# Left sweeps: GpSimd's residual additions in pieces of 256 columns, one per half step, released by VectorE's remainder

## The reference, cut to what matters

```python
x = x + L0(_gn(x))      # a convolution whose weights are mixed per sample
x = x + L1(_gn(x))      # four sweeps: down, up, right, left
x = x + L2(_gn(x))      # linear attention and a depthwise convolution
x = x + L3(_gn(x))      # four sweeps again
```

```python
def step(prev, row):
    new = row + jax.nn.relu(_conv1d(prev, w, b))   # 64 -> 64 channels, 9 taps
    return (new, new)
```

## Time and profile before

| what | value |
|---|---|
| median of three runs | 3067.09 us |
| the profiled execution: its own time | 3078.55 us |
| its span in the trace | 3076.7 us |
| TensorE busy (matmul) | 2698.7 us, 88% |
| VectorE busy | 2166.5 us, 70% |
| ScalarE busy | 1361.2 us, 44% |
| GpSimd busy | 298.9 us, 10% |
| mean granted TensorE clock | 0.945 of full speed |

### The profile page before, as it was taken

How to read it: one execution, slowest core, us unless ns; L and a number is a source line. 1 busy time by engine, 2 the same in 40 slices (tenths; PEclk the granted TensorE clock), 3 DMA queues, 4 the chain that set the end, 5 groups by cost and what they waited for, 6 DMA issues and landing times. The chain is left out here.

```text
span 3076.7 us, 71764 instructions
## 1 busy us (share of the span) xinstructions
PE 2698.7 (88%) x25712; PEld 2429.3 (79%) x25712; DVE 2166.5 (70%) x5168; ACT 1361.2 (44%) x2113; POOL 298.9 (10%) x816
## 2 busy tenths in 40 slices
PE   5888879999999999928978888886999999999791
PEld 4666669999999999923457676666999999999791
DVE  7888856776667677767028887886766767677865
ACT  2777642246642222236445565652225663222120
POOL 1112110000000011135000100010000000000602
PEclk9998989999999999958989999998999999999695
DMA  4333320000000000079247888777000000000759
GB/s 91 83 83 87 91 113 0 0 0 0 0 0 0 0 0 0 0 222 230 48 42 88 108 101 101 98 91 120 0 0 0 0 0 0 0 0 0 124 94 130
DMA packets 735623, 164.91 MB, mean 54 GB/s; under 512 B 728208, under 2 KB 728848, under 8 KB 730640
## 3 DMA queue, kind: packets, MB, share of 16 engines
q1 hardware_dynamic: 608640, 132.08, 24.8%
q10 hardware_dynamic: 126864, 31.19, 6.2%
HBM read 96.13 MB, written 67.11 MB: 53 GB/s over the span
## 5 line engine op out<-in xcount | busy, mean ns | idle before, releaser
L271 PE MATMUL L_conv<-L_x_hi,L_w_hi 128*128 128x248 f32 (+2 forms) x5040 | 1218.1, 279 | 51.1 <-DVE L_w_lo L234 29.1
L271 PE MATMUL L_conv<-L_x_hi,L_w_lo 128*128 128x248 f32 (+2 forms) x5040 | 1209.7, 279 | 0.0
L158 ACT ACTIVATE L_row_b<-S,L_bias 128x256 f32 (+1 forms) x1008 | 513.4, 510 | 1120.2 <-DVE L_x_hi L212 1109.8
L271 PEld LDWEIGHTS L_conv<-L_x_hi,L_w_hi 128*128 128x128 f32 x5040 | 959.1, 190 | 55.3 <-issue 29.2
L271 PEld LDWEIGHTS L_conv<-L_x_hi,L_w_lo 128*128 128x128 f32 x5040 | 960.6, 191 | 0.0
L222 DVE SCALAR_TENSOR_TENSOR S<-L_conv,L_neg_bias,L_row_b 128x256 f32 x1008 | 487.3, 483 | 446.1 <-PE L_conv L276 445.8
L276 PE MATMUL L_conv<-L_x_lo,L_w_hi 128*128 128x248 f32 (+2 forms) x5040 | 750.8, 279 | 6.6 <-DVE L_x_lo L214 6.6
L276 PEld LDWEIGHTS L_conv<-L_x_lo,L_w_hi 128*128 128x128 f32 x5040 | 659.5, 191 | 10.3 <-DVE L_x_lo L214 9.9
L214 DVE TENSOR_TENSOR L_x_lo<-S,L_x_hi 128x256 fp32r<-128x256 f32 x1016 | 466.5, 459 | 34.7
L212 DVE TENSOR_SCALAR L_x_hi<-S 128x256 fp32r (+1 forms) x1016 | 320.8, 316 | 41.4 <-PEq L47 6.2
L607 PE MATMUL dc_conv<-dc_xz_hi,dc_w_hi 128*128 128x512 f32 x384 | 170.8, 445 | 6.5 <-DVE dc_w_lo L734 6.5
(11 more groups left out here) (202 smaller groups left out, 2829.1 us busy)
## 6 DMA issues: line engine op xcount, KB each, us to landing
dc_raw<-x SPq DMA_DIRECT2D x32, 512.0 KB, 6.6
x_scratch<-dc_raw SPq DMA_DIRECT2D x16, 1024.0 KB, 7.5
at_res<-x_scratch SPq DMA_DIRECT2D x32, 512.0 KB, 11.7
x_scratch<-at_res SPq DMA_DIRECT2D x64, 256.0 KB, 5.8
fs_buf<-x_scratch SPq DMA_DIRECT2D x32, 512.0 KB, 6.7
sh_G<-x_scratch ACTq DMA_DIRECT2D x56, 256.0 KB, 6.0
out<-fs_buf SPq DMA_DIRECT2D x32, 256.0 KB, 4.4
out<-fs_buf ACTq DMA_DIRECT2D x32, 256.0 KB, 4.8
```

The costliest lines, as they stand in the source:

```text
L158: nc.scalar.activation(row_b[p][:, :, :], line(k, at_step(k, i), p), ACT.Identity, bias=bias[:, k:k + 1]).then_inc(row_b_ready[p], 1)
L271: nc.tensor.matmul(out[:, to, :], w[:, k, s * P:(s + 1) * P], x_hi[p][:, at, :], start=(s == PADJ and n == 0), stop=False)
```

## The change

Both classes take a function `split_done(i, p)` instead of the semaphore `new_ready`: it makes GpSimd wait for `lo_ready[p]` of step `i` in the left sweep, that is, until VectorE has written the remainder of that half step. Every addition is cut by rows into pieces of 256 elements per partition, and each piece waits for a half step of its own.

In L1's left sweep a quarter's five additions become ten pieces (16 of the 32 row pairs each). Piece `half` of sample `n` waits for half step (15 + n, half), (31 + n, half) or (47 + n, half). The statistics wait for twice the count. In L3's left sweep an item becomes four pieces (`PIECES`, 8 row pairs each), and the 64 pieces wait for the half steps (31, 0), (31, 1), (32, 0) and so on up to (62, 1), the sweep's last. SP waits for four pieces before it stores an item. Nothing is changed in `final_sum`.

```diff
             if final:
-                final.early_pool(pool, new_ready, done_before)
+                def split_done(i, p):
+
+                    pool.wait_ge(lo_ready[p], turns_before(3, i) + 2)
+
+                final.early_pool(pool, split_done)
...
-    def add_quarter(self, eng, n, g):
+    def add_quarter(self, eng, n, g, rows=slice(0, J)):
         part = slice(g * QUARTER, (g + 1) * QUARTER)
-        cells = self.xr[n][:, :, part]
-        return eng.tensor_tensor(cells, cells, columns_of(self.S, n)[:, :, part], ALU.add)
+        cells = self.xr[n][:, rows, part]
+        return eng.tensor_tensor(cells, cells, columns_of(self.S, n)[:, rows, part], ALU.add)
...
-    def early_pool(self, pool, new_ready, done_before):
+    def early_pool(self, pool, split_done):
         for n in range(RING):
             pool.wait_ge(self.x1_in[n], 16)
         for g in (3, 2, 1):
-            for p in range(2):
-                pool.wait_ge(new_ready[p], done_before(3, STEPS - g * QUARTER))
             for n in range(RING):
-                self.add_quarter(self.nc.gpsimd, n, g).then_inc(self.quarter_summed, 1)
+                for half in range(2):
+                    split_done(STEPS - g * QUARTER + n, half)
+                    self.add_quarter(self.nc.gpsimd, n, g, slice(half * J // 2, (half + 1) * J // 2)).then_inc(self.quarter_summed, 1)
...
-                dve.wait_ge(self.quarter_summed, (3 - g) * RING + n + 1)
+                dve.wait_ge(self.quarter_summed, 2 * ((3 - g) * RING + n + 1))
...
+PIECES = 4
...
-            sp.wait_ge(self.early_summed, item + 1)
+            sp.wait_ge(self.early_summed, PIECES * (item + 1))
...
-    def early_pool(self, pool, new_ready, done_before):
-        for p in range(2):
-            pool.wait_ge(new_ready[p], done_before(3, STEPS - PART))
+    def early_pool(self, pool, split_done):
         for item in range(B):
             pool.wait_ge(self.loaded[item % BUFS], 16 * (item // BUFS + 1))
-            self.add(self.nc.gpsimd, item).then_inc(self.early_summed, 1)
+            for piece in range(PIECES):
+                split_done(STEPS - PART + (item * PIECES + piece) // 2, piece % 2)
+                self.add(self.nc.gpsimd, item, slice(piece * J // PIECES, (piece + 1) * J // PIECES)).then_inc(self.early_summed, 1)
```

More of the change, by code:

```diff
@@ L1769, in store, with add @@
                           self.buf[item % BUFS][q * HALF:(q + 1) * HALF, :, :]).then_inc(self.stored[item % BUFS], 16)
-    def add(self, eng, item):
-        buf = self.buf[item % BUFS]
-        return eng.tensor_tensor(buf[:, :, :], buf[:, :, :], columns_of(self.S, item % B)[:, :, self.columns(item)], ALU.add)
+    def add(self, eng, item, rows=slice(0, J)):
+        cells = self.buf[item % BUFS][:, rows, :]
+        return eng.tensor_tensor(cells, cells, columns_of(self.S, item % B)[:, rows, self.columns(item)], ALU.add)
     def early_sync(self, sp):
```

## The result

| | median | runs |
|---|---|---|
| before | 3068.08 us | 4, 3066.92 to 3072.22 |
| after | 3035.23 us | 4, 3025.99 to 3042.10 |

The ratio is 0.9881, with a 95% interval from 0.9856 to 0.9906. The change makes the kernel 1.2% faster, by 32.9 us where 34.9 were forecast, and 3035 us against 3032. (The median of before is that of four runs, one more than the forecast started from.) The difference is well beyond the 0.2%, 6 us, within which the prediction would have called it no change. The profiled execution of after took 3042.10 us (span 3040.3).

What follows compares the result with a forecast made beforehand. GpSimd's whole additions were taken to hold back VectorE's rounding and remainder, so that TensorE waits in the left sweeps. From 3067.09 us, -9.65 (L1), -35.6 (L3) and +10.3 (end) make -34.9, 3032 us; range 3025 to 3047.

Steps and rivals of the forecast that it cites:

- What bounds it, and what goes: L1's and L3's left sweeps: GpSimd additions hold back rounding and remainder; pieces in the gaps win 9.65 and 35.6 us.
- Does a piece fit: Gap from remainder to next rounding: 0.965 us on average, less 0.14 for the start, for a piece of 0.80 us.
- the prediction's sum: Each piece in the left sweeps: start delay plus length beyond the 0.965 us gap is overrun; 0.8 us per group free.
- the line through 512 and 1024 elements: GpSimd's additions: a line through 1.56 and 2.95 us gives 0.87 us for a piece of 256 elements.
- the 512 row: GpSimd's addition of 512 elements: 1.56 us, said to include a wait for VectorE at its start.
- the rivals for long pieces: Both left sweeps: pieces of 1.05 us give 3050 us (chance 0.13), pieces of 1.56 us give 3098 us (0.04).
- What comes: End of L3's left sweep: SP's two stores and three loads before the barrier delay the final sum, +10.3 us.
- the chain of store, landing and load: End of L3's left sweep: load 28 waits for item 15's stores, the second landing 4.4 us after issue.
- the lower bound: End of L3's left sweep: only load 28's wait for item 15's stores counts, +7.4 us.
- a cheap end: End of L3's left sweep: SP's issues go through fast, some 3 us are left, 3025 us; chance 0.05.
- The sum: Whole kernel: -9.65 and -35.6 us in the left sweeps, +10.3 at the end, -34.9 us in all.
- the prediction's range: Whole kernel: from 3025 us (little cost at the end) to 3047 us (costlier end and most of the too-long case).

Runs made afterwards that it cites:

- e5: The changed kernel with L3's items in 2 pieces of 512 elements, each released by half 0's remainder of every step: 3043.4 us, 0.9909 of before.
- e6: The changed kernel with L3's items whole (1024 elements), each released by a remainder, one in two steps: 3058.2 us, 0.9948 of before.
- e10: The changed kernel with L3's items in 3 pieces of 352 or 320 elements, one per half step: 3030.1 us, 0.9866 of before.
- e4: The changed kernel with item 15's stores and the loads of items 26 to 28 moved behind the barrier: 3033.0 us, 0.9863 of before.
- e3: The changed kernel with L3's pieces run one behind the other after step 30, none waiting for a remainder: 3025.7 us, 0.9851 of before.
- e8: The changed kernel with L3's items cut by columns, 8 at a time, added as early as they are final: 3023.8 us, 0.9840 of before.
- e9: The changed kernel with the pieces of both L1 and L3 back to back, none waiting for a remainder: 3036.4 us, 0.9880 of before.
- e7: The changed kernel with every piece in both left sweeps released by its half step's maximum instead of the remainder: 3036.4 us, 0.9880 of before.

## Why the prediction was right

**What bounds it, and what goes.** The view was right: whole additions that exclude the rounding and the remainder one for one. The two gains were forecast at 9.65 and 35.6 us and measured at 9.8 and 35.6. The clock stays at 1.00, as forecast. L1's statistics do not wait.

**Does a piece fit.** Yes, but partly by luck. I took 0.80 us for a piece and 0.14 us for its start. The trace shows 0.87, and 0.08 for three pieces in four, so two errors cancel and these end 0.95 us behind the remainder, for 0.94 forecast. The fourth, the first piece of each item, has a load to wait for as well, starts 0.14 us behind and ends at 1.01, past the gap of 0.92 that it lies in: its record ends 0.08 to 0.10 us behind the start of the next rounding. By the prediction's sum these roundings would be late. None is: no rounding under the pieces takes over 0.30 us. The prediction had nothing for this overlap. Of its bounds for a piece, the line through 512 and 1024 elements (0.87) was the right one; that the 512 row held a wait was wrong, since e5's pieces of 512 take 1.55 us undisturbed.

**The slack.** Here a step was wrong: "TensorE needs the rounded part only about 0.8 us after it is ready". It is about 0.4 us (e5, e6 and the row of TensorE). In the forecast nothing hung on it, since no rounding was late; in the rivals for long pieces each group of pieces would have cost 0.4 us more. Their price per piece was wrong the other way: for e10's 48 pieces, 1.10 us on average, the prediction's sum gives 48 x (1.10 + 0.14 - 0.965) - 0.8 = 12.4 us, and the sweep lost 4.1.

**What comes.** Forecast +10.3 us, measured +10.9. The stores took 1.6 us (I had 2), the loads 7.9 us. e4 shows that SP's five issues hold the barrier, and e3, e8, e9 and e10 show that the cost is gone once the additions end early. But the chain of store, landing and load, on which the lower bound and the case against a cheap end rested, did not bind: item 15's second store had landed at 2970.97, and load 28 was issued at 2972.74, right behind load 27. What took the time were the issues themselves, 1.8, 3.0 and 3.0 us for the three loads.

**The sum.** -34.9 us forecast, -34.6 in the stages of the profiles, -32.9 between the medians. The last two differ by less than the interval of the ratio, some 7.7 us to either side. The largest spread that the profiles show without an edit is that of the part in the middle, which the prediction's range did not name.

**What it did not see.** The prediction put the whole gain down to pieces that lie in the gaps. e3 shows that the same pieces without any release lose only 5.1 us in L3, because a collision costs as much as one piece is long and TensorE has slack for part of it. The release, which was half of the change, costs more as it is placed here (10.9 us) than it brings (5.1 in L3 and 1.5 in L1). That 94 pieces stand in front of 94 roundings is a small danger at this size: without any release they cost 6.6 us in both sweeps (e9).

## What to carry to other kernels

Where two engines exclude each other instruction by instruction, cut the instructions of the one that isn't urgent first: the length of one bounds the price of a collision, and a delay below the slack of the bounding engine (0.39 us here) costs nothing. Pace them afterwards, and look at what the pacing pushes against the next barrier; work that trickles to the end of a stage drags its stores and loads with it. Read slack from the bounding engine's own next instruction, its weight load included, not from that of the engine which waits for its result.

## What the runs showed of the hardware

- A GpSimd addition of two SBUF operands took 0.869 us for 256 elements per partition, 1.55 for 512 and 2.85 to 2.89 for 1024, undisturbed or nearly so. The pattern of access (8 rows of 32, 32 rows of 8, 16 of 16) made no difference above 0.01 us.
- GpSimd started 0.08 us behind the VectorE instruction that released it, be it the remainder (after) or the maximum (e7). Pieces that also had a load to wait for, one in four in after and all in e6, started 0.14 to 0.15 us behind it, as the first addition of before did.
- A VectorE instruction held back by GpSimd seems to move before the end of GpSimd's record: in e7 the remainder of 2880.84 ends at 2881.81, so that with its usual 0.43 us it ran from 2881.38, while the piece's record (0.97 us from 2880.56) ends at 2881.53, 0.15 us later. In after every fourth piece's record ends 0.08 to 0.10 us behind the start of a rounding that is not late.
- With some microseconds of rest before, SP issued a pair of stores of 256 KB in 1.6 us and the load of 512 KB behind them in 1.8 us; a second and a third load right behind took 3.0 us each (after, end of the sweep).
